# Layer four attention: where the second maximum's products of a score slot stand in TensorE's order

## The reference, cut to what matters

```python
qh = q.reshape(b, s, KVH, G, D).transpose(0, 2, 3, 1, 4)   # KVH 8, G 4, D 8
kh = k.reshape(b, s, KVH, D).transpose(0, 2, 1, 3)
scores = jnp.einsum('bkgsd,bktd->bkgst', qh, kh) * scale
attn = jax.nn.softmax(scores, axis=-1) / DROPOUT
out = jnp.einsum('bkgst,bktd->bkgsd', attn, vh)
```

## Time and profile before

| | before |
|---|---|
| median of 3 runs | 805.28 us (804.13 to 806.03) |
| profiled execution, its own time | 806.28 us |
| its span | 804.3 us |
| TensorE busy in the span | 700.3 us (87%) |
| VectorE busy | 538.4 us (67%) |
| ScalarE busy | 352.6 us (44%) |
| granted TensorE clock, mean | 0.953 |

### The profile page before, as it was taken

One profiled execution on the slowest core, in us unless ns is written; L12 is line 12 of the kernel. 1 busy time (PEld: TensorE's weight loads), 2 busy tenths in 40 slices (PEclk: granted clock), 3 DMA queues, 4 the chain that ended last, 5 costly groups with the idle time before them and its releaser, 6 DMA issues. The chain is left out here.

```text
span 804.3 us, 14007 instructions
## 1 busy us (share of the span) xinstructions
PE 700.3 (87%) x4485; PEld 466.5 (58%) x4485; DVE 538.4 (67%) x1627; ACT 352.6 (44%) x622; POOL 214.5 (27%) x307
## 2 busy tenths in 40 slices
PE   9999997988988887698787888978788999999995
PEld 4643466765764665487665776754233328776774
DVE  6786888788773888858873453456886957524554
ACT  2662445455454755232123423425478793212220
POOL 0002585001000122112312551553144220342340
PEclk9999998999999999879999999998699999999999
DMA  6996421040000230000061151011000053132315
GB/s 190 344 207 126 150 73 53 4 159 1 2 3 0 69 91 1 1 1 7 34 230 40 42 185 32 14 61 52 29 2 2 4 161 57 38 108 80 106 60 177
DMA packets 55566, 60.24 MB, mean 75 GB/s; under 512 B 13847, under 2 KB 48808, under 8 KB 55496
## 3 DMA queue, kind: packets, MB, share of 16 engines
q1 hardware_dynamic: 50408, 46.02, 20.6%
q0 software_dynamic: 4848, 13.28, 4.7%
q10 hardware_dynamic: 240, 0.05, 0.0%
HBM read 34.92 MB, written 24.20 MB: 74 GB/s over the span
## 5 line engine op out<-in xcount | busy, mean ns | idle before, releaser
L1953 ACT ACTIVATE arenas<-psum 128x512 f32<-128x512 f32 (+6 forms) x89 | 63.2, 732 | 59.3 <-PE psum L1160 50.5
L3181 DVE TENSOR_REDUCE arenas<-psum 128x2 f32<-128x512 f32 x96 | 61.9, 684 | 12.0 <-PE psum L1732 10.5
L969 POOL TENSOR_SCALAR arenas<-arenas,small 128x1024 f32<-128x1024 f32 x8 | 9.0, 1122 | 160.3 <-DVE small L2920 160.3
L986 POOL DMA_INDIRECT experts_l<-shared,small x30 | 29.1, 969 | 80.8 <-ACT shared L2253 72.2
L1149 PE MATMUL psum<-conb 128*128 128x512 bf16 x167 | 43.2, 403 | 4.9 <-ACT early L1953 3.1
L1160 PE MATMUL psum<-con,early 128*128 128x128 f32 (+1 forms) x188 | 33.3, 287 | 15.7 <-ACT late L1953 4.4
L1160 PE MATMUL psum<-conb,shared 128*128 128x128 bf16 (+2 forms) x512 | 38.7, 229 | 8.8 <-issue 3.9
L3146 DVE TENSOR_TENSOR shared<-shared,psum 128x128 f32<-128x128 f32 x30 | 8.6, 288 | 53.6 <-PE psum L1685 26.7
L1160 PEld LDWEIGHTS psum<-conb,shared 128*128 128x128 bf16 (+2 forms) x512 | 33.5, 118 | 17.1 <-issue 14.4
L1953 ACT ACTIVATE late<-psum 128x512 f32<-128x512 f32 (+1 forms) x51 | 25.6, 501 | 40.3 <-PE psum L1160 40.3
L2300 ACT ACTIVATE early<-psum 128x1024 f32<-128x1024 f32 x32 | 31.9, 1031 | 17.1 <-PE psum L1749 17.1
(11 more groups left out here) (436 smaller groups left out, 1785.5 us busy)
## 6 DMA issues: line engine op xcount, KB each, us to landing
sorted_l<-late SPq DMA_DIRECT2D x3, 1920.0 KB, 18.4
early<-sorted_l SPq DMA_DIRECT2D x6, 645.0 KB, 5.8
early<-in_L_ffn_sw SPq DMA_DIRECT2D x3, 1024.0 KB, 9.3
late<-sorted_l SPq DMA_DIRECT2D x23, 129.0 KB, 2.1
sorted_l<-late SPq DMA_DIRECT2D x1, 2944.0 KB, 25.1
early<-in_L_ffn_We_gate_up SPq DMA_DIRECT2D x2, 1408.0 KB
early<-in_L_ffn_expert_w SPq DMA_DIRECT2D x2, 1024.0 KB, 6.5
early<-in_L_ffn_w SPq DMA_DIRECT2D x1, 2048.0 KB, 8.3
```

Source lines behind the costliest of these rows:

```text
L986: pool.indirect_dma_start(expert_rows2[p], bass.IndirectOffsetOnAxis(dest2[p][:, i:i + 1], 0), out_r2[k], None).then_inc(outs_sent[k], 16)
L1953: act.activation(dst, view(v), ACT.Copy, scale=scale).then_inc(f.drained(i, key), 1)
L3181: dve.tensor_reduce(nm, q3d(f.slot(0, ("max", w, k)), 2, S), X, ALU.max, negate=True)\
```

## The change

In each slot the loop took one maximum behind the scores and one at the slot's end. It now takes both directly behind the scores. In an odd slot the values therefore follow the second maximum, where they stood between the two; in a slot with columns the columns do so too. In an even slot without columns nothing moves. No instruction is added or removed, and the other engines' orders and the banks stay what they were.

```diff
                     exp3(w, m)
-                    next(maxima, None)
+                    for _ in range(2):
+                        next(maxima, None)
                     for at, key in inserts3[w]:
                         if at == m:
                             turn_columns3(*key)
                     if g >= 3 and g % 2 == 1:
                         pair = (g - 3) // 2
                         values3(pair // 4, pair % 4)
-                    next(maxima, None)
                     if m == 4 and w > 0:
                         tokens3(w - 1)
```

## The result

The changed kernel takes 812.36 us in the median of 5 runs (806.93 to 814.70), the kernel before 805.55 (804.13 to 809.61) in the runs beside it. The ratio is 1.0063, with a 95% interval of 1.0033 to 1.0093: slower by about 5.1 us, between 2.7 and 7.5. (The interval belongs to this ratio, which is not the quotient of the two medians; those lie 6.8 apart.) The forecast was 809.2, in a range of 805.0 to 812.6. Both kernels spread by several us, so the place of the loss has to be read from traces and not from single times. Two of the kernels further down had one execution each in a slower state of the chip (827.16 and 817.76 us), which counts in their medians and not in their ratios. The profiled execution of the changed kernel, 806.93 us with a span of 804.9, is the fastest of its five.

A forecast was written before the change was run, and what follows sets the result against it. With three engines near their limits, the order of waits decides, VectorE pacing plain units. Terms 0.9 + 1.0 + 0.98 + 0.34 + 0.73 = 3.95, say 3.9 us, on 805.28 give 809.2; range 805.0 to 812.6, forecast's own 807.8 to 810.8.

The forecast's parts named there:

- The signs named beforehand: Odd slots: second maximum waits on VectorE, values right behind; VectorE idle before k8, k0, k12; units 2, 4, 6 start later.
- The mechanism: Odd slots: second maximum waits for its bank with values and next scores queued behind; VectorE 0.22 us short per slot.
- the walk: Step-by-step timing of the unit's 16 maxima, k0 to k15 (slot m holds k2m and k2m+1), through banks and engines.
- Units 4 and 5: Plain units: unit 4 costs 0.34 us on VectorE, unit 5 costs 0.73 because its scores are handed to unit 6.
- Units 2 and 3: Scores reach unit 3 0.73 us late, ScalarE's copies pass it on; k0 reaches VectorE 0.98 us later in all.
- Units 0 and 1: Unit 0, last odd slot at half clock: 0.9 us; unit 1, values displaced and columns 0.91 and 0.99 late: 1.0 us.
- The count of odd slots: Units 0 to 5: second maximum moves ahead of the values in 24 odd slots, four per unit.
- the third rival: The rival Pairing pays: 0.22 us freed in each of 24 slots, 5.3 us, cut to 3.3; chance 0.14.
- Unit 6: After the last maxima: ScalarE's chain of exponentials begins with the late scores, so unit 5 is charged the full 0.73 us.
- The clock rises later: Unit 0: a wait ahead of k15 delays full clock, unit 1 runs at half clock; adds 2 to 4 us; chance 0.12.
- The lateness is absorbed: Slot loop: hand-overs are quicker than walked, only phases move; result within 1.6 us; chance 0.18.
- Pairing pays: Odd slots: TensorE is the true limit and paired maxima share time; 3.3 us faster, 802.0; chance 0.14.

The follow-up runs named there:

- the first fill: Nine unread constant matmuls ahead of unit 1's shift, added to each order; against the kernel before: old order 804.67 us (0.9993), new order 811.63 us (1.0083).
- both fills: Unread constant matmuls ahead of unit 1's shift and in slot waits of units 0 and 1; against the kernel before: old order 805.23 us (0.9996), new 810.79 (1.0039).
- the quarter reductions: VectorE reduces only a quarter of each score row in units 2 to 7; against the kernel before: old order 796.93 us (0.9894), new order 799.59 (0.9940).

## Why the prediction was right or wrong, point by point

**The number** came out inside the range of 805.0 to 812.6, but by 0.24 us, and outside the forecast's own 807.8 to 810.8. The difference of 5.1 us lies within the forecast 2.5 to 5.5; the difference of the medians, 6.8, does not. In the first two profiles the loop lost 3.39 us where 3.95 were forecast. That this is so close is in part luck, for the terms missed to both sides: unit 0 by +0.42, unit 1 by -1.45, units 2 to 5 by +0.47. The signs named beforehand did appear: the loop's end moved by more than 1.6 us, and units 4 and 5 became longer (22.40 to 23.52). The changed profile's loop starts 1.19 us earlier (558.12 and 559.31); with that added, units 2, 4 and 6 begin at 597.7, 626.2 and 649.7, where 598.8, 627.2 and 650.2 were forecast.

**The mechanism** was right and is shown for the plain units: a bank wait behind which values and next scores stand. The profile has it at the odd slots of unit 5 (waits of 0.35, 0.34, 0.21 and 0.35 us), with VectorE's idle at 0.22, 0.23 and 0.82 where the walk said 0.22, 0.22 and some 0.8. The 0.62 us of idle before k11 went nowhere: it turned into the idle before k12.

**Units 4 and 5** were mis-sized, and this is the term that the traces pin down. Follow the start of k0's reduction. In unit 4 it is late by 0.98 us against unit 2's first scores (28.08 before, 29.06 now), as forecast. From there to unit 5's k0 the forecast had 0.34, and 0.57 were lost (11.18 to 11.75). From unit 5's k0 to unit 6's first scores it had 0.73, and 0.97 were lost (10.15 to 11.12). The whole of units 2 to 5 is 2.52 where the terms add up to 2.05. I walked one unit from k4 on and took the part ahead of it as unchanged. After the values that follow k3, the next scores, the shift's transposes (639.76) and then k4 (639.98) have to be formed: k0 to k4 takes 3.03 us (637.37 to 640.40), where it took 2.80. That is the missing 0.23 in each of the two units, the same shortfall as at k8 and k0.

**Units 2 and 3** were put at 0.98 on VectorE, which is what was measured; the scores' part of that walk was 1.41 at unit 4's start, and measured it is 1.40 (27.02 to 28.42 us).

**Units 0 and 1**, 0.9 and 1.0: measured against their partners in the same group, unit 0 is longer by 1.33 and unit 1 by 0.98 (the change in units 0 and 1 alone), with the first fill by 1.29 and 0.79. The match of 0.98 with 1.0 does not confirm the walk through unit 1: of that pair the changed kernel has 13.6 us of half clock in unit 1 and its partner 6.8. The walk put the first two turns of columns 0.91 and 0.99 later. At mostly full clock, with both fills, they come 0.23 and 0.32 later from unit 1's start, and the unit is 0.33 longer; the fills stand in that unit's waits too. So unit 1's term stays open, and likely too large. In the two profiles compared first, unit 1 became shorter, by 0.45. There VectorE's additions of results into x (line 3166) took 1.25 and 0.86 us for two each, in the changed kernel, and 2.00 and 1.43 in the kernel before, at another moment of GpSimd's work:

```profile
580.23 1.25 DVE L3166 SCALAR_TENSOR_TENSOR xs<-arenas,dispatch,xs 128x256 f32<-128x256 f32 x2
```

```profile
580.26 2.00 DVE L3166 SCALAR_TENSOR_TENSOR xs<-arenas,dispatch,xs 128x256 f32<-128x256 f32 x2
```

These 1.32 us, taken with the 0.45, would give a loss of 0.87. That GpSimd is what slows them is argued from their overlap and not shown.

**The count of odd slots** was wrong: unit 0's first odd slot has no values, so 23 were displaced and not 24. No term used the number but the third rival's.

**Unit 6** starts 3.39 us late but is 0.22 us shorter, so a little of the hand-over comes back; I had passed it on whole.

**The rivals.** *The clock rises later* did not happen in unit 0 of the changed kernel, where the granted clock rose at about the same place (0.53 over 560 to 580 in both). Half clock that comes back within unit 1 does occur, in both orders. Its own share is open: the traces give 0.7 to 2.3 us for units 0 and 1 and 2.3 for the rest (2.52 less unit 6's 0.22), so 3.0 to 4.6, where the two groups measured 5.1 (2.7 to 7.5) and 4.6 (2.3 to 6.8). Nothing demands a further cause, and the intervals would hide one of a microsecond or two; the part ahead of the loop, above, is where one could lie. *The lateness is absorbed* is refuted by the units' lengths. *Pairing pays* is refuted as a net gain. The four maxima's matmuls do take 0.38 us where a pair had free banks (646.00), so the concurrency is real; but in the old order the second maximum already ran beside the next scores, which begin in the other half of the rows. In the kernel before, this row stands beside the maximum of the earlier trace rows at 643.80:

```profile
643.80 0.39 PE L1749 MATMUL psum<-late 50*128 50x512 bf16 x1
```

And with the quarter reductions, where VectorE is mostly idle, the new order's only gain is the 0.25 us around the turned sums, less than it loses elsewhere in the unit.

## What to carry to other kernels

When a producer writes through a small ring of banks, count the items that it forms in a row against the ring: the one that comes round waits for the full round trip (write, read, release), and all work placed behind it in the same order waits too. In this kernel independent work was better put inside that round trip, between the items, than behind them; paired matmuls were worth less than the time that such filler hid. Read an idle stretch of the consumer with the one behind it: removing 0.62 us before one item only moved it to the next, which had its own reason to be late.

## What the runs showed of the hardware

The length of a stage of four units with three engines in step, 49.4 us in the old order and 51.9 in the new, repeated to 0.02 us in five profiles each, on several chips. One more profile had half clock in the stage and took 54.2. The whole kernel with full reductions spread by 5 to 13 us between runs of the same program. Much of that spread goes with the granted clock: over 35 runs of the kernel before, in each of two groups, time and mean clock correlate with -0.8, though the means lie between 0.941 and 0.957 in all of them. The part ahead of the loop took 557.6 to 560.2 us in four profiles of the old order, with 48 to 51 us at half clock, and 569.1 in the longest of all, on another chip, with 65. Nine matmuls in an idle of 1.94 us did not keep the clock at its 2.4 GHz level: it fell 3.8 us after them, in an idle of 2.92 us.
